# Two transformer layers with routed experts: layer 0's biases as matmuls, 31 and 23 blocks a round, scatters that wait for one another

## The reference

```
xn = layernorm(x);  x = x + attn0(xn) + shared0(xn) + moe0(xn)     # 16 experts of width 64
xn = layernorm(x);  x = x + attn1(xn) + moe1(xn)                   # 8 experts of width 352
attn: 16 heads of 8;  layer 0: q, gate, k, v = xn @ W + b, rmsnorm of q and k per head,
      softmax(q k / sqrt(8)) v, times sigmoid(gate), @ Wo + bo;  layer 1: no bias, gate, norm or Wo
moe:  probs = softmax(xn @ Wr); the two largest of each token pick its experts;
      y = sum over both of weight * (silu(xn @ Wg) * (xn @ Wu)) @ Wd
```

## Time and profile before

| | us |
|---|---|
| runs, median (lowest to highest) | 693.94 (688.59 to 694.24) |
| profiled execution, its own time | 687.82 |
| its span (work on the core) | 686.0 |
| PE busy | 643.7 (94%) |
| DVE busy | 502.2 (73%) |
| ACT busy | 450.7 (66%) |
| POOL busy | 308.7 (45%) |
| PE's share of the chain that ended last | 75% |
| mean granted PE clock | 0.973 |

### The profile page before, as it was taken

The page is one execution under the profiler, slowest core; times in us unless marked ns, Lnnn a source line. Parts: engine busy times, 40 slices in busy tenths (PEclk is TensorE's granted clock), DMA queues, the critical chain, the costliest instruction groups (busy, mean ns, idle before and its releaser), DMA issues.

```text
span 686.0 us, 13133 instructions
## 1 busy us (share of the span) xinstructions
PE 643.7 (94%) x4200; PEld 352.8 (51%) x4200; DVE 502.2 (73%) x1088; ACT 450.7 (66%) x843; POOL 308.7 (45%) x422
## 2 busy tenths in 40 slices
PE   2999987999999999898999999899999999999986
PEld 1876742654544454333466566555656555656221
DVE  3699779787778798777858777876677777666732
ACT  2443258777768878565877676666667667666774
POOL 3256844873155635646482122666365122122550
PEclk9999998999999999799999999899999999999997
DMA  8954216365344434336645444444755554431110
GB/s 232 295 151 146 84 50 184 118 202 158 103 134 135 149 118 127 102 90 197 212 118 175 146 152 132 145 144 141 219 182 164 161 164 134 140 93 37 47 48 16
DMA packets 82965, 95.16 MB, mean 139 GB/s; under 512 B 7249, under 2 KB 70097, under 8 KB 82897
## 3 DMA queue, kind: packets, MB, share of 16 engines
q1 hardware_dynamic: 78800, 85.91, 41.7%
q0 software_dynamic: 4096, 8.40, 4.2%
HBM read 67.68 MB, written 26.21 MB: 137 GB/s over the span
## 4 chain that ended last, share of the span: by engine, by line
PE 75%; DVE 9%; issue 4%; DMA 3%; POOL 3%; ACT 3%; SPq 2%; another core or an unknown queue 1%; POOLq 0%; DVEq 0%; ACTq 0%
PE pv_ps L917 15%; PE slot L888 15%; PE slot L905 13%; PE slot L865 9%; PE slot L878 6%; PE pv_ps L779 5%; DVE mx L1285 3%; PE slot L854 2%; PE slot L925 2%; PE slot L847 2%; DMA wbuf<-in_experts 1%; PE slot L790 1%; PE slot L897 1%; ACT probsT L1047 1%
## 5 line engine op out<-in xcount | busy, mean ns | idle before, releaser
L1285 DVE TENSOR_REDUCE mx<-slot 128x1 f32<-128x512 f32 x512 | 334.9, 685 | 117.7 <-PE slot L888 94.3
L1047 ACT ACTIVATE probsT<-slot 128x512 f32<-128x512 f32 x512 | 284.2, 597 | 90.4 <-PE slot L905 71.7
L888 PE MATMUL slot<-k_stack,q_stack 72*128 72x512 bf16 x512 | 197.9, 387 | 9.6 <-DVE mx L1285 7.9
L905 PE MATMUL slot<-q_stack,k_stack 75*128 75x512 bf16 x512 | 194.6, 390 | 9.4 <-issue 3.6
L917 PE MATMUL pv_ps<-probsT,v 128*32 128x512 f32 x1024 | 140.5, 621 | 0.9 <-ACT probsT L1047 0.8
L1379 POOL TENSOR_TENSOR hid<-th,up 128x512 f32<-128x512 f32 (+2 forms) x56 | 71.2, 1271 | 130.5 <-DVE th L1148 76.6
L888 PEld LDWEIGHTS slot<-k_stack,q_stack 72*128 72x128 bf16 x512 | 50.1, 98 | 131.8 <-issue 74.7
L1367 POOL DMA_INDIRECT yg<-ys_hbm,index x64 | 62.2, 972 | 45.5 <-issue 34.1
L865 PEld LDWEIGHTS slot<-xgT,wbuf 128*128 128x128 f32 (+1 forms) x576 | 75.6, 186 | 12.3 <-issue 1.1
L905 PEld LDWEIGHTS slot<-q_stack,k_stack 75*128 75x128 bf16 x512 | 50.2, 99 | 58.0 <-issue 19.0
L1356 POOL DMA_INDIRECT xs_hbm<-xn,index x64 | 64.0, 1000 | 32.4 <-DVE index L1262 16.4
(11 more groups left out here) (133 smaller groups left out, 605.5 us busy)
## 6 DMA issues: line engine op xcount, KB each, us to landing
wbuf<-in_experts SPq DMA_DIRECT2D x48, 544.0 KB, 4.9
q_stack<-parts_hbm SPq DMA_DIRECT2D x96, 96.0 KB
k_stack<-parts_hbm SPq DMA_DIRECT2D x96, 96.0 KB
wbuf<-in_experts SPq DMA_DIRECT2D x64, 128.0 KB, 2.7
xg<-xs_hbm SPq DMA_DIRECT2D x28, 256.0 KB
ys_hbm<-ys SPq DMA_DIRECT2D x28, 256.0 KB, 2.6
parts_hbm<-parts SPq DMA_DIRECT2D x16, 384.0 KB
xs_hbm<-zeros SPq DMA_DIRECT2D x2, 2048.0 KB, 12.6
```

Source lines behind the costliest of these rows:

```text
L888: nc.tensor.matmul(ps[:, 0:N], q_stack[0:STACK, h, j * P:(j + 1) * P], k_stack[0:STACK, h, :], start=True, stop=True).then_inc(slot_full, 1)
L905: nc.tensor.matmul(ps[:, 0:N], k_stack[0:STACK + MAXROWS, h, j * P:(j + 1) * P], q_stack[:, h, :], start=True, stop=True).then_inc(slot_fu ...
L1047: nc.scalar.activation(probsT[:, k % PROBS, a, :], ps[:, 0:N], ACT.Exp, scale=SCALE).then_inc(slot_free, 1)
L1285: nc.vector.tensor_reduce(mx[:, g, u // J, u % J:u % J + 1], ps[:, 0:N], AXIS.X, ALU.max)\
```

## The change

1. The biases are cut in three bf16 parts that lie in rows 0, 64 and 96 of a tile. A second matmul of each QV bank, with a matrix that has ones in these three rows, adds them to the bank. ACT now empties the bank with three activations: the squares, a copy of queries and keys, a copy of values, gate and logits. DVE's two additions and the stage SQ are gone.
2. A round has 31 and 23 blocks, so that the last group of a round has three, and every loop and width follows `live(r, q)`.
3. On POOL, a pair of scatters, and likewise a pair of gathers, waits until all the earlier pairs of its round have landed.
4. PE starts after the first memsets; only its first transpose waits for the first loads. WARM stages may so stand ahead of it.
5. The planner has a new table, offsets for single groups of heads (EDGE), and new assumed durations for the changed stages.

```diff
-NB = (32, 24)
+NB = (31, 23)
...
-WARM = 196
+WARM = 229
...
+def live(r, q):
+
+    return min(4, NB[r // 2] - 4 * q)
...
-            pe.wait_ge(first_in, 64)
-            pe.wait_ge(consts_set, 4)
+            pe.wait_ge(zeros_set, 1)
...
                     nc.tensor.matmul(ps[:, 0:2 * D + VGW[0]], xnT[:, A % 2, j * P:(j + 1) * P], w_tok[:],
-                                     start=True, stop=True).then_inc(slot_full, 1)
+                                     start=True, stop=False)
+                    nc.tensor.matmul(ps[:, 0:2 * D + VGW[0]], pick[:], bias_parts[:],
+                                     start=False, stop=True).then_inc(slot_full, 1)
...
-                    for b in range(4):
+                    for b in range(live(r, q)):
                         for c in range(CHUNKS[l]):
...
+                elif kind == "QV":
+                    A, j = stage[1:]
+                    sc.wait_ge(*filled(stage))
+                    if A >= 1:
+                        sc.wait_ge(parts_done, 2 * A)
+                    two = slice(2 * j * D, 2 * (j + 1) * D)
+                    nc.scalar.activation(squares[:].rearrange("p a t -> p (a t)")[:, two], ps[:, 0:2 * D], ACT.Square)
+                    nc.scalar.activation(qk_tok[:, two], ps[:, 0:2 * D], ACT.Copy)
+                    nc.scalar.activation(vgl[:, J * seq(A) + j, :], ps[:, 2 * D:2 * D + VGW[0]], ACT.Copy)\
+                        .then_inc(slot_free, 1)
...
+                    if A == 0:
+
+                        link(nc.vector.tensor_copy(bias_parts[:], bias_tok[:]))
+                        link(nc.vector.tensor_tensor(bias_tok[64:P], bias_tok[64:P], bias_parts[64:P], ALU.subtract))
+                        link(nc.vector.tensor_copy(bias_parts[64:P], bias_tok[64:P]))
+                        nc.vector.tensor_tensor(bias_parts[96:P], bias_tok[96:P], bias_parts[96:P], ALU.subtract)\
+                            .then_inc(bias_set, 1)
...
+                    if k:
+                        gp.wait_ge(scattered[r], 2 * 16 * k)
                     for ab in range(2):
...
+                    if k:
+                        gp.wait_ge(yg_in[r], 2 * 16 * k)
                     for ab in range(2):
```

More of the change, by code:

```diff
@@ L131, in moments @@
             t = GROUPS[r][0] + GROUPS[r][1] * q
-            for b in range(4 * q, 4 * q + 4):
+            for b in range(4 * q, 4 * q + live(r, q)):
                 put(t + LAG["WL"][l], "WL", r, b)
@@ L262, in tasks @@
                 before = [(pe, ("QK", A - 1, a)) for a in range(2)] + [(dve, ("SS", A - 1))] if new and j == 0 else []
[L263 to L267, removed]
+                add(pe, ("QV", A, j), 0.88, 1.1, (act, ("XT", A)), *before, chain="QV")
+                add(act, ("QV", A, j), 0.92, 1.05, (pe, ("QV", A, j)), new and (parts_by(A - 1), ("PT", A - 1, 1)), chain="QV")
+            add(dve, ("SS", A), 1.87, 1.97, (act, ("QV", A, J - 1)), new and (dve, ("NM", A - 1)))
             add(act, ("SS", A), 3.2 if new else 0.5, 3.3 if new else 0.6, (dve, ("SS", A)), new and (dve, ("NM", A - 1)))
@@ L323, in tasks @@
             add(dve, ("XA", A), 0.65, 0.75, (dve, ("AT", A, G - 1)))
-            add(sp, ("OUT", s), 0.4, 4.0, (dve, ("XA", A)), (dve, ("YC", 2 + s // 2, s % 2)))
+            add(sp, ("OUT", s), 0.4, 4.0, s == B - 2 and (sp, ("NT", 2 * B - 1, G - 1)), (dve, ("XA", A)), (dve, ("YC", 2 + s // 2, s % 2)))
+    at["zeros", 0] = 0.0
+    add("IN", ("zeros", 0), 0.1, 5.6)
     for i in range(WARM):
-        add(pe, ("WARM", i), 0.22, 0.22, (pe, ("XT", 0)), chain="WARM")
+        add(pe, ("WARM", i), 0.22, 0.22, ("IN", ("zeros", 0)), chain="WARM")
     for r in range(4):
@@ L374, in tasks @@
             r, q = rest
-            add(pe, stage, 0.92, 1.2, (act, ("XG", r, q)), (sp, ("WL", r, 4 * q + 3)), chain="gated")
+            add(pe, stage, 0.23 * live(r, q), 0.3 * live(r, q), (act, ("XG", r, q)), (sp, ("WL", r, 4 * q + live(r, q) - 1)), chain="gated")
         else:
@@ L1003, in _ @@
                         sc.wait_ge(h_done, n - 1)
-                    nc.scalar.activation(th[0:rows, n % 2, :], ps[0:rows, 0:N], ACT.Tanh, scale=0.5)\
+                    w = N if kind == "SG" else live(*stage[1:3]) * P
+                    nc.scalar.activation(th[0:rows, n % 2, 0:w], ps[0:rows, 0:w], ACT.Tanh, scale=0.5)\
                         .then_inc(th_done, 1)
@@ L1011, in _ @@
                         sc.wait_ge(h_done, n - 1)
-                    nc.scalar.activation(up[0:rows, n % 2, :], ps[0:rows, 0:N], ACT.Copy, scale=0.5)\
+                    w = N if kind == "SU" else live(*stage[1:3]) * P
+                    nc.scalar.activation(up[0:rows, n % 2, 0:w], ps[0:rows, 0:w], ACT.Copy, scale=0.5)\
                         .then_inc(slot_free, 1)
@@ L1073, in _ @@
                 nc.vector.memset(probs[l][:], NOT_THERE)
-            link(nc.vector.memset(hid[64:P], 0.0))
+            nc.vector.memset(hid[64:P], 0.0)
+            link(nc.vector.memset(pick[:], 0.0))
+            for row in (0, 64, 96):
+                last = nc.vector.memset(pick[row:row + 1], 1.0)
+            link(last)
             ve.wait_ge(first_in, 64)
```

110 lines of the change are left out of this document (52 added, 58 removed).

## The result

The changed kernel takes **714.28 us** (median of four runs, 705.13 to 715.2) where the kernel before, beside it on the same chip, takes 692.98: a ratio of 1.029, with a 95% interval of 1.019 to 1.039. It is slower, by 2 to 4%. The forecast was 671 us, in a range of 653 to 693.

The account below looks back on a forecast made before the run. DVE's chain was taken to bound the span up to the first PV, PE the rest, with a stall besides. 687.82 - 12 - 8 + 5 - 4 = 669, plus 2 for spread, gave 671 us, range 653 to 693.

Parts of the forecast that it names:

- The waits on POOL: Scatter and gather pairs waiting for earlier ones: +5 us, +3 at the end and +2 for MPs, bounds 0 and +33.
- The cover: On POOL, busy for 45%, most of the added waiting hides, except at the end; 23 of 64 pairs directly follow another.
- The landing: On POOL, a pair directly behind another costs 1.3 to 4.1 us more.
- The slower rival: MP behind runs of waiting pairs holds PE at NT: 37 us more, 701 us, up to 706 with slow clock; chance 0.12.
- The stalls: DVE's unnamed waits behind the first PV, 5.5 us, and PE's slow clock end if indirect DMA bursts cause them: -4 us.
- The rival by which waiting removes no traffic: On POOL, landings as long as the gather's; stalls stay and the end is 13 us late: 684 us, chance 0.20.
- The start: Up to the first PV: banks, SQ, SL, SW, scatters and a stall go from ahead, some work comes late: -12 us.
- my lower bound: At the start, only 2 us gained if QV banks on ACT or the DMAs of the parts hold the first M.
- One block less: On PE behind the first PV, one block less a round and work moved ahead: -8 us, bounds -10.5 and -3.
- The biases and banks: PE's added matmuls cost 0, at worst +2.9 us; ACT's 14 to 29 us more are covered by its idle time.
- The end: Round 3's last gathers and YC end some 4 us late, behind the last attention result: +3 us.
- work and order: The gain apart from waits and stalls: the start at -12 us and one block less at -8, -20 together.

Follow-up runs that it names:

- h2: The changed kernel, unaltered with all 56 waits, timed again beside the kernel before: 713.4 us, 1.029 of before.
- h1: The changed kernel without any pair waits (e1 again), in a set where stalls occur: 692.2 us, 0.997 of before.
- f5: The kernel before, unaltered, run again for its trace in a set without stalls: 667.0 us, one run, beside 666.7.
- e1: The changed kernel with both pair waits taken out, order kept, in a set without stalls: 655.5 us, 0.986 of before.
- e4: The changed kernel with the old order numbers and no pair waits, 31 and 23 blocks: 683.7 us, 1.029 of before.
- f2: e4 with 32 and 24 blocks a round again instead of 31 and 23: 687.3 us, 1.032 of before.
- i1: g3 with 32 and 24 blocks a round instead of 31 and 23: 710.4 us, 1.026 of before.
- g3: The changed kernel with waits ahead of every second pair alone, 24 instead of 56: 677.8 us, 0.975 of before.
- h4: The kernel before with waits ahead of every second pair, 24 in all: 678.9 us, 0.980 of before.

## Why the prediction was wrong

**The waits on POOL** are the step that failed: "+5 us, bounds 0 and +33" against 48 us where no stalls are. Where they are, h2 less h1 gives 21 us, with the stalls that the waits end already taken off. Three parts of it were wrong.
- The cover, above all ("so most of this hides"). It did not hide: PE stood 33.8 us more. And I let only the 23 pairs that follow another directly wait. 20 of these did, for 55 us, but so did 23 others, for 31 us: what stands between two pairs, an MP of 1.4 us or a GA of 1.3, is as short as the landing.
- The landing. I bounded it by 1.3 and 4.1 us. Where a pair directly follows another, the 20 waits have a mean of 2.8 us, within that, and a median of 2.0. The Trainium skill's fixed 2.0 us (DMA: Bandwidth & Descriptors, Anatomy of one DMA) agrees with the median. But they reach 5.6 and 6.4 us, and PE's three longest waits (7.2, 3.9 and 3.0 us) each stand behind one of 4.4 us or more.
- The clock. Of the 52 us in PE's windows 18 are no idle time but slower matmuls (0.96 against 0.99), as behind the stop shown above. I gave the slower case 5 us for that.

The slower rival (701 us, chance 0.12) named the mechanism: MP behind a run of waiting pairs, PE at NT behind MP. The products of the experts (GA), which hold up DN and, in the longest wait, ACT, it left out. "POOL's idle half speaks against it" was the wrong reading: a wait that is in order ahead of MP and GA is not covered by the engine's idle time elsewhere, since the instructions with a deadline stand behind it. Even that case priced 37 us, because it counted nine waits.

**The stalls** were read rightly in kind: they come with bursts of indirect DMAs, the pair wait ends them, and the "remote" row went. What exactly stops the engines no trace shows. The rival by which waiting removes no traffic, so that the stalls stay, fell; what the Trainium skill says of shared DMA engines (DMA: Bandwidth & Descriptors, Issuing engines are not separate DMA queues) may hold, but the stalls don't follow from it. Their size is not the kernel's alone. With four of them the span of before is 686.0, without, in f5, 665.1. Of these 21 us PE stands 10.8 more and works 10.1 longer on the same 4200 matmuls. My terms had 4.3 + 4.

**The start** was -12; the first PV came 7 us earlier (93.19 to 86.21), outside the 79 to 83 that I named. 4.3 of it is the stall, so that the work brought 2.7, and 3.8 in e1 against f5 (88.16 to 84.41). MP came 6.4 us earlier, not 12.1. The first M began at 48.42 us (48.13 before), having waited 1.54 us for its DMA: that was the condition of my lower bound, and the 5.7 us of eight banks and SQ, which stand ahead of the first M, brought it no earlier. I had also misread the timeline of DVE: the banks of three sequences, not two, stood ahead of the 16th maximum, those of A = 2 among the maxima (from 64.83 us). From MP to the first PV it took 17.5 us, 3.7 longer than before without its stall of 4.3 (13.8): about the 4 us that I had counted.

**One block less** was -8. From the first PV to the end of the span e1 takes 567.1 us and f5 576.9, so 9.8 less, and PE's busy time there falls by 10.0 against my 10.5. But as a term of its own it does not exist: by the ratios it is 2 us between e4 and f2, and 36 between i1 and g3. I had taken the order as fixed and the blocks as work that drops out of it.

**The biases and banks** were right: PE's additional matmuls hide, and PE waits no longer for exponentials (1.6 us in e1, 2.3 in f5). ACT got 9 us more rather than 14 to 29: a bank's three activations take 0.72 us when they follow one another, 11.5 in all, and two table loads of 1.28 us fell away. **The end** was +3 and is about that.

Within one set, where stalls occur: before 693.9; work and order -1.7 (h1: 692.2), where I had -20; the waits +21.2 (h2: 713.4). So the gain of work and order was a miss too: new order and fewer blocks came to 10.4 us where no stalls are (e1) and to almost nothing where they are. That fits the stops: on "remote" ACT waits 28 us in h1 and 12.6 in the trace of before. Across the sets the same 713.4 is made up of before 693.9, work and order -11.2 (655.5 against 666.7), the waits +48.0 and the stalls that stay away -17.3. The last is the 27.2 that before is slower where they occur less the 10.0 that the changed kernel is. Those 10.0 us have no unnamed wait behind them and stay open.

The best version found is the changed kernel with 24 waits: 0.975 and 0.971 of before, against 1.029 with 56 and 0.997 with none. The one with 16, at 0.976, can't be told from it, and the kernel before with 24 (h4, 0.980) hardly. All were timed only where stalls occur; for a chip without them the cost of 24 waits was not measured.

## What to carry to other kernels

Price a wait on an in-order engine by what stands behind it and when that is due, not by the engine's idle share; count every wait whose cover is shorter than the longest landing seen, and add the slow clock behind each stop of TensorE. A throttle on a queue may not need a wait at every step: with 16 or 24 of the 56 here the kernel was faster (0.971 to 0.976) than with all or none, and POOL stood 25 to 28 us in them instead of 86.5. And where a planner writes the order from durations, its numbers and the code are one thing: each half alone cost 3 to 5.5% here.

## What the runs showed of the hardware

- The same kernel takes 666 us in two sets and 688 to 694 in three and beside the result. In the slow ones DVE and ScalarE stop, mostly together, several times, DVE for 0.6 to 4.3 us each, in or just behind runs of four or more indirect DMAs that POOL issues 1.26 us apart; in the fast ones the same runs pass without a stop. Two sets of different kinds bear the same chip number, so it is not settled that the chip itself decides.
- With a wait ahead of every pair no such stop was seen in five traces, two of them where before has the stops. With one ahead of every second pair, 3 or 4 stops of DVE are left, each at a run of four or more.
- A pair of indirect DMAs of 128 rows each held the pair directly behind it for 1.5 to 6.4 us from the end of its issue, 2.0 at the median (20 waits). During the longest, from 551 to 558 us, the DMA engines were busy for 71% and moved 202 GB/s, against 129 over the span; whether that is the cause was not tested.
